# Weaving 18 of 32 gathers between the first six scatters on GpSimd

## The chip, the cores and the metric

One core of a Trainium2 chip runs the kernel. The metric is device time in microseconds (us), as the median of several executions. One more execution was taken with the hardware profiler; its trace is what all rows below come from.

## What is computed

The input `x` is 16 images of 128 channels and 16 x 16 pixels, so 4096 tokens of 128 numbers.

```python
x = x + einsum('oc,bchw->bohw', W, _ln_c(x))      # W from 32 Householder vectors
t = _to_tokens(x)                                  # 4096 tokens
xf = _ln_t(t)
Sm = softmax(xf @ W_router + b_router)             # 32 experts
G_ek, idx_ek = top_k(Sm.T, 128)                    # each expert takes its 128 best tokens
tokens = xf[idx_ek]
act = silu(einsum(tokens, W_up[group]) + b_up)     # 8 groups of 4 experts, width 341
Eout = einsum(act, W_down[expert]) + b_down
y = zeros.at[idx_ek].add(G_ek * Eout)              # tokens can be taken by several experts
out = _from_tokens(t + y)
```

## The kernel before

All arithmetic is in one program with five instruction streams (SyncE, GpSimd, ScalarE, VectorE, TensorE), ordered by semaphores alone; each stream is written out by hand and executes in its order.

The first part, up to about 67 us of the trace, makes the convolution, both normalisations, the softmax and the threshold of each expert. It leaves the normalised tokens with their 32 gate values in a DRAM table `token_rows` of 4096 rows of 160 floats, and two DRAM tables `acc0` (the residual) and `acc1` (zeros).

The second part goes over the 32 experts.

- TensorE finds the token numbers of an expert with a small matmul (`find`, L1152), VectorE turns its result into `idx[:, e]` (`token_number`, L944 and L946). The first 16 are made in a row; the other 16 are made four at a time between later units.
- GpSimd gathers the 128 rows of expert `e` from `token_rows` with an indirect DMA (`gather`, L523) into its own slot `xg[:, e, :]`; the slot of one expert is never used by another. It waits for `idx` of that expert alone.
- The experts are worked in nine units: experts 0-1, 2-3, and then 4-7, 8-11, 12-15, 16-19, 20-23, 24-27, 28-31. Of each unit TensorE transposes the gathered rows (`gathered_transpose`, L1164, after the wait for all gathers of the unit), multiplies with the up weights (`up`, L1178) and with the down weights (`down`, L1194). ScalarE copies the transposed rows (L650) and applies silu (L659). VectorE multiplies the down result with the gate and leaves `eo[:, e, :]`, which is the space of `X` (L991).
- The results of experts 0 to 25 (`SCATTERED` = 26) go back by an indirect DMA of GpSimd that adds to DRAM (`scatter`, L532), in turn into `acc1` and `acc0`. Scatter `e` waits for `eo` of its expert and for the landing of all earlier scatters to the same table, which is that of `e - 2`.
- The results of experts 26 to 31 go back through TensorE: VectorE makes a one-hot matrix of the token numbers for each (`token_onehot`, L956, four pieces each), and TensorE multiplies it with three bf16 parts of the result into all eight PSUM banks (L1216, 6 experts x 24 matmuls).

The end: when the scatters to `acc1` have landed, ScalarE's queue starts four loads of it (L663); when both tables are complete, SyncE's queue starts the other loads (L453, L454). VectorE adds the two tables chunk by chunk (L1001, eight chunks), TensorE transposes each sum onto the accumulated banks (L1221), ScalarE copies the banks out (L666), SyncE stores them (L457, L460).

On TensorE the order of a step `k` is `up(k + 1)`, `gathered_transpose(k + 2)`, `down(k)`; after the last `down` come L1216 and L1221. On VectorE the multiplications L991 of a unit come after the `token_number` calls of the next unit's finds, and pieces of L956 stand between them.

What sets the order on GpSimd in the second part is `AHEAD`: `AHEAD` gathers are issued before the first scatter. Before, `AHEAD` is 32, so all gathers come first and then the 26 scatters.

Of the kernel before, what the change touches and what calls it, by code (L numbers as in the profile page):

```python
# [10 lines left out]
E = 32  # L11
# [57 lines left out]
HOT_AFTER = (10, 17, 25)  # L69

INTO = tuple((SCATTERED - 1 - e) % 2 for e in range(SCATTERED))
AHEAD = E
EARLY = 4


# [50 lines left out]
def metaformer_block(nc, x, V, w_router, b_router, w_up, b_up, w_down, b_down, c32, c16, ch16, ccol, out):  # L126
# [7 lines left out]
    with ctx:  # L134
# [329 lines left out]
        def _(pool):  # L464
# [56 lines left out]
            def gather(e):  # L521
                pool.wait_ge(s_idx, e + 1)
                nc.gpsimd.indirect_dma_start(  # L523
                    out=xg[:, e, :], out_offset=None, in_=rows[:, :],
                    in_offset=bass.IndirectOffsetOnAxis(ap=idx[:, e:e + 1], axis=0)).then_inc(s_g[UNIT_OF[e]], 16)

            def scatter(e):
                pool.wait_ge(s_eo, e + 1)
                i = INTO[e]
                if e >= 2:  # L530
                    pool.wait_ge(s_sc[i], 16 * INTO[:e].count(i))
                nc.gpsimd.indirect_dma_start(  # L532
                    out=acc[i][:, :], out_offset=bass.IndirectOffsetOnAxis(ap=idx[:, e:e + 1], axis=0),
                    in_=eo[:, e, :], in_offset=None, compute_op=ALU.add).then_inc(s_sc[i], 16)
# [7 lines left out]
                in_offset=bass.IndirectOffsetOnAxis(ap=row_number[:, 0:1], axis=0)).then_inc(s_first, 16)  # L542
            for e in range(AHEAD):
                if e == E - 1:
                    pool.wait_ge(s_first, 16)
                gather(e)
            e = 0
            while e < SCATTERED:
                scatter(e)
                e += 1  # L550
# [691 lines left out]
```

## Time and profile before

| | us |
|---|---|
| median of 3 runs | 196.4 (196.19 to 196.7) |
| profiled execution, its own time | 196.68 |
| span of its trace | 194.9 |
| TensorE busy | 139.9 (72% of the span) |
| GpSimd busy | 107.1 (55%) |
| VectorE busy | 108.9 (56%) |

The span runs from the first to the last instruction, and 1.8 us of the profiled execution's own time lie around it. Times in rows count from the span's start. In rows PE is TensorE, PEld its weight loads, DVE VectorE, ACT ScalarE, POOL GpSimd, SP SyncE. The mean granted clock of TensorE is 0.828 of full speed. A busy GpSimd says that it makes DMA descriptors; the transfer itself runs on the DMA engines afterwards.

### The profile page before, as it was taken

The page shows a single profiled execution, that of the slowest core. Times are in us where ns is not written, and L with a number is a line of the kernel's source. Part 1 is how long each engine was busy: PE and PEld are TensorE (multiplying, and loading weights), DVE is VectorE, ACT ScalarE, POOL GpSimd, SP SyncE. Part 2 cuts the span into 40 slices and gives each one's busy share as a digit, 9 for nine tenths or more (in the row PEclk, how much of TensorE's full clock was granted, in tenths as well). Part 3 has the DMA queues.
Part 4 walks back from the last instruction along what each step waited for, and adds up shares of the span by engine and source line. Part 5 has one row for each costly group of instructions (what it writes and reads, how often), then busy time and mean ns, then how long its engine had stood idle before and what let it go on. Part 6 is the DMA issues. An engine that isn't in the chain of part 4 may idle for free.

```text
span 194.9 us, 2467 instructions
## 1 busy us (share of the span) xinstructions
PE 139.9 (72%) x694; PEld 87.6 (45%) x697; DVE 108.9 (56%) x433; ACT 76.1 (39%) x266; POOL 107.1 (55%) x120
## 2 busy tenths in 40 slices
PE   0999965413215347754299997999974999999990
PEld 0557954301104224334134763777652344444690
DVE  2454998984676692110435448458399069945500
ACT  3166899536895675100234252335400000000161
POOL 2028478997560277774356377878768878600000
PEclk9999999955555555557579999999997599999997
DMA  4999999999867062222112223334343333399666
GB/s 96 300 335 309 293 294 208 249 403 285 221 185 217 17 265 70 64 62 60 31 36 50 50 54 42 31 27 40 27 42 28 27 32 39 28 290 344 240 212 222
DMA packets 31982, 28.39 MB, mean 146 GB/s; under 512 B 6784, under 2 KB 25680, under 8 KB 31840
## 3 DMA queue, kind: packets, MB, share of 16 engines
q1 hardware_dynamic: 25777, 22.74, 39.8%
q0 software_dynamic: 5328, 4.41, 15.3%
q10 hardware_dynamic: 864, 1.08, 1.7%
q8 instruction: 6, 0.10, 0.2%
q14 instruction: 7, 0.06, 0.1%
HBM read 17.61 MB, written 10.62 MB: 145 GB/s over the span
## 4 chain that ended last, share of the span: by engine, by line
PE 53%; DVE 14%; POOL 12%; another core or an unknown queue 7%; issue 6%; ACT 3%; DMA 2%; SPq 0%; POOLq 0%; DVEq 0%
PE PZ L1216 9%; PE PT L1178 7%; PE PM L1178 6%; PE PZ L1194 5%; PE PT L1216 4%; PE PM L1216 4%; POOL rs L493 4%; PE PM L1194 3%; POOL rs L486 3%; PE PT L1017 3%; DVE wdn L956 2%; POOL act L499 2%; PE PZ L1221 2%; PE PT L1164 2%
## 5 line engine op out<-in xcount | busy, mean ns | idle before, releaser
L532 POOL DMA_INDIRECT acc<-X,idx x26 | 40.8, 1567 | 12.2 <-issue 8.2
L523 POOL DMA_INDIRECT xg<-token_rows,idx x32 | 30.4, 951 | 21.0 <-issue 9.6
L956 DVE TENSOR_SCALAR_CACHE_REDUCE wdn<-wide,slot_token 128x1024 bf16<-128x1024 f16 x24 | 29.9, 1273 | 7.0 <-PE PZ L1216 7.0
L944 DVE TENSOR_SCALAR_CACHE_REDUCE junk<-PZ,k 128x128 f16<-128x128 f32 x24 | 8.3, 348 | 25.1 <-remote 13.2
L666 ACT ACTIVATE X<-PZ 128x512 f32<-128x512 f32 x4 | 2.4, 598 | 45.1 <-PE PZ L1221 45.1
L1065 PE MATMUL PZ<-stage_w,X 128*128 128x192 f32 x64 | 14.7, 382 | 6.9 <-DVE act L788 6.5
L1194 PE MATMUL PZ<-wdn,act 128*128 128x128 f32 x132 | 18.7, 290 | 1.0 <-DVE X L991 1.0
L1194 PEld LDWEIGHTS PZ<-wdn,act 128*128 128x128 f32 x132 | 17.3, 204 | 2.1 <-DVE X L991 1.4
L1178 PE MATMUL PM<-xgT,wup 128*128 128x512 f32 (+3 forms) x26 | 15.0, 667 | 3.6 <-issue 2.5
L659 ACT ACTIVATE act<-PT,bup 128x512 f32<-128x512 f32 (+3 forms) x14 | 9.0, 641 | 21.4 <-PE PT L1178 14.5
L1178 PE MATMUL PT<-xgT,wup 128*128 128x512 f32 (+3 forms) x28 | 16.4, 672 | 0.9 <-ACT xgT L650 0.9
L659 ACT ACTIVATE act<-PM,bup 128x512 f32<-128x512 f32 (+3 forms) x13 | 8.3, 637 | 21.0 <-remote 8.1
L1065 PEld LDWEIGHTS PZ<-stage_w,X 128*128 128x128 f32 x64 | 12.4, 224 | 8.3 <-DVE act L788 7.5
L1216 PE MATMUL PZ<-wdn,S 128*128 128x512 bf16 x47 | 14.2, 406 | 2.5 <-DVE X L991 2.5
L1152 PE MATMUL PZ<-cum,onehot 32*128 32x129 f16 x32 | 6.9, 256 | 11.1 <-DVE idx L946 6.0
L991 DVE TENSOR_SCALAR X<-PZ,xg 128x128 f32<-128x128 f32 x22 | 7.4, 348 | 12.0 <-PE PZ L1194 10.1
L1152 PEld LDWEIGHTS PZ<-cum,onehot 32*128 32x128 f16 x32 | 2.9, 96 | 23.9 <-issue 20.5
L588 ACT ACTIVATE act<-act,mn 128x32 f32<-128x32 f32 x32 | 9.8, 310 | 6.0 <-DVE mn L792 6.0
L751 DVE SCALAR_TENSOR_TENSOR x<-PZ,rs,xg 128x128 f32<-128x128 f32 x32 | 9.1, 343 | 4.3 <-PE PZ L1065 2.7
L493 POOL TENSOR_TENSOR rs<-ve,mhalf 128x4 f32<-128x4 f32 x8 | 8.1, 1007 | 3.7 <-DVE ve L773 3.7
L620 ACT ACTIVATE xf<-x,shift,rs 128x128 f32<-128x128 f32 x24 | 9.4, 483 | 0.0
L1001 DVE TENSOR_TENSOR x<-x,xf 128x512 f32<-128x512 f32 x8 | 5.5, 693 | 6.9 <-DMA x<-acc 6.9
(180 smaller groups left out, 280.2 us busy)
## 6 DMA issues: line engine op xcount, KB each, us to landing
X<-in_x SPq DMA_DIRECT2D x8, 256.0 KB, 5.3
acc<-zero SPq DMA_DIRECT2D x4, 512.0 KB, 6.7
acc<-x SPq DMA_DIRECT2D x8, 256.0 KB, 5.9
token_rows<-xf SPq DMA_DIRECT2D x8, 256.0 KB, 2.3
x<-acc SPq DMA_DIRECT2D x8, 256.0 KB, 5.8
out<-X SPq DMA_DIRECT2D x3, 512.0 KB, 3.6
wup<-in_L_ffn_W_up SPq DMA_DIRECT2D x1, 1364.0 KB, 7.8
wdn<-in_L_ffn_W_down SPq DMA_DIRECT2D x1, 1280.0 KB
```

What stands on the lines that cost most here:

```text
L493: link(nc.gpsimd.tensor_tensor(rs2[:, g, :], ve2[:, g, :], mhalf[:, :], ALU.pow))
L523: nc.gpsimd.indirect_dma_start(out=xg[:, e, :], out_offset=None, in_=rows[:, :], in_offset=bass.IndirectOffsetOnAxis(ap=idx[:, e:e + 1], a ...
L532: nc.gpsimd.indirect_dma_start(out=acc[i][:, :], out_offset=bass.IndirectOffsetOnAxis(ap=idx[:, e:e + 1], axis=0), in_=eo[:, e, :], in_off ...
L588: ins = nc.scalar.activation(pr[:, g, u, :], lg[:, g, u, :], ACT.Exp, bias=mn[:, g, u:u + 1], scale=-1.0, accum_out=sm[:, g, u:u + 1])
L620: ins = nc.scalar.activation(xf[:, t, :], x1[:, t, :], ACT.Identity, bias=shift2[:, g, u:u + 1], scale=rs2[:, g, u:u + 1])
L659: nc.scalar.activation(act[0:fn, k % 2, j, 0:n * P], src, ACT.Silu, bias=bup[0:fn, j, e0 // PER:e0 // PER + 1]).then_inc(s_act, 1)
L956: nc.vector.tensor_scalar(hot(k)[:, r], columns[:, r], slot_token[:, k:k + 1], None, ALU.is_equal, ALU.add, accum_out=found_in[:, k * HOT_ ...
L1065: ins = mm(PZ[:, 2 * (g % 2) + u // 2, (u % 2) * W_:(u % 2 + 1) * W_], X[:, g, u * P:(u + 1) * P], stage_w[:, :], start=True, stop=True)
L1152: mm(find_bank(e), onehot[r, g, :], cum[r, g, 0:P + 1], start=True, stop=True).then_inc(s_find, 1)
L1178: mm(dst, wup[:, e0 // PER, f0:f0 + fn], xgT[:, k % 2, 0:n * P], start=True, stop=True).then_inc(s_up, 1)
L1194: ins = mm(down_bank(e), act[0:rows_, k % 2, j, q * P:(q + 1) * P], w, start=(j == 0), stop=(j == 2))
L1216: ins = mm(out_bank(g), parts[j][:, k, :], hot(k)[:, g * 512:(g + 1) * 512], start=(k == 0 and j == 0), stop=False)
```

## The change

The gathers are no longer all issued first. GpSimd issues gathers 0 to 13, then scatter 0 and gathers 14, 15, 16, then scatter 1 and gathers 17, 18, 19, and so on up to scatter 5 and gathers 29, 30, 31; the 20 scatters 6 to 25 follow in a row. The gathers, the scatters and their own semaphore waits are the same instructions in another order. One wait is no longer issued: that of gather 31 for an earlier gather into the same slot (`s_first`), which stands in the first loop alone.

```diff
-AHEAD = E
+AHEAD = 14
+PER_SCATTER = 3
@@
             for e in range(AHEAD):
                 if e == E - 1:
                     pool.wait_ge(s_first, 16)
                 gather(e)
-            e = 0
+            e, ahead = 0, AHEAD
+            while ahead < E:
+                scatter(e)
+                for _ in range(PER_SCATTER):
+                    gather(ahead)
+                    ahead += 1
+                e += 1
             while e < SCATTERED:
                 scatter(e)
                 e += 1
```

## Rows read from the trace of the kernel before

**Rows 1.** The page, chain that ended last, share of the span by engine.
```profile
PE 53%; DVE 14%; POOL 12%; another core or an unknown queue 7%; issue 6%; ACT 3%; DMA 2%; SPq 0%; POOLq 0%; DVEq 0%
```

**Rows 2.** The chain in order of time: start us, us, what.
```profile
80.41 5.09 another core or an unknown queue
...
86.07 6.47 another core or an unknown queue
...
93.12 1.57 another core or an unknown queue
...
182.87 0.43 PE PZ L1216 x2
183.30 1.78 PE PZ L1221 x16
```

**Rows 3.** Timeline of POOL: start us, us, instruction, count, [idle before <-what ended it].
```profile
84.68 0.95 POOL L523 DMA_INDIRECT xg<-token_rows,idx  x1 [0.30 <-issue]
...
89.69 0.95 POOL L523 DMA_INDIRECT xg<-token_rows,idx  x1 [0.30 <-issue]
...
115.94 0.95 POOL L523 DMA_INDIRECT xg<-token_rows,idx  x1 [0.49 <-issue]
117.19 1.62 POOL L532 DMA_INDIRECT acc<-X,idx  x1 [0.31 <-DVE X L991]
...
168.28 1.55 POOL L532 DMA_INDIRECT acc<-X,idx  x1 [0.45 <-issue]
```

**Rows 4.** Lines L523 and L532: duration in ns (least/median/most), first and last start.
```profile
L523 POOL DMA_INDIRECT xg<-token_rows,idx x32: 943/948/1027, 68.4 to 115.9; - x32
...
L532 POOL DMA_INDIRECT acc<-X,idx x26: 1552/1552/1681, 117.2 to 168.3; - x26
```

**Rows 5.** Timeline of DVE, first gated results of the experts.
```profile
96.92 0.61 DVE L991 TENSOR_SCALAR X<-PZ,xg 128x128 f32<-128x128 f32 x2 [1.07 <-remote]
...
103.17 0.35 DVE L991 TENSOR_SCALAR X<-PM,xg 128x128 f32<-128x128 f32 x1 [0.16 <-PE PM L1194]
```

**Rows 6.** Timeline of PE from the first to the last transpose of gathered rows.
```profile
73.59 0.66 PE L1164 MATMUL PT<-k,xg 128*128 128x128 f32 x2 [1.06 <-DMA xg<-token_rows,idx]
...
87.32 2.77 PE L1194 MATMUL PZ<-wdn,act 128*128 128x128 f32 x12
...
96.31 2.08 PE L1178 MATMUL PT<-xgT,wup 128*128 128x512 f32 x2
...
105.11 1.12 PE L1178 MATMUL PT<-xgT,wup 128*128 128x512 f32 x2
...
107.50 0.66 PE L1164 MATMUL PT<-k,xg 128*128 128x128 f32 x4
...
121.62 0.60 PE L1164 MATMUL PT<-k,xg 128*128 128x128 f32 x4
...
127.46 0.60 PE L1164 MATMUL PT<-k,xg 128*128 128x128 f32 x4
...
133.31 0.60 PE L1164 MATMUL PT<-k,xg 128*128 128x128 f32 x4
```

**Rows 7.** DMA issues of 60 to 80 us: last number is median us from issue to landing.
```profile
xg<-token_rows,row_number POOLq DMA_INDIRECT x1, 2.8
```

**Rows 8.** Timelines of the queues of ACT and SP, then of DVE, at the end.
```profile
169.68 1.79 ACTq L663 DMA_DIRECT2D xf<-acc  x4
...
172.20 1.76 SPq L454 DMA_DIRECT2D x<-acc  x4
...
176.21 1.42 DVE L1001 TENSOR_TENSOR x<-x,xf 128x512 f32<-128x512 f32 x2 [3.52 <-DMA x<-acc]
...
184.45 0.69 DVE L1001 TENSOR_TENSOR x<-x,xf 128x512 f32<-128x512 f32 x1 [0.58 <-DMA x<-acc]
```

**Rows 9.** Stage 92 to 96: busy us and count of PE, PEld, DVE, ACT, POOL; clock; DMA share, GB/s.
```profile
92.00:96.00 4.00, 0.00 (x0) 0.00 (x0) 1.59 (x8) 1.02 (x2) 1.42 (x2) 0.69 0.08 20
```

## The prediction

> **What bounds the kernel now.** I read the chain that ended last first, then the timelines of GpSimd, TensorE and VectorE from 68 us on, then the queues at the end. TensorE has over half of the chain and GpSimd 12% [rows 1]; from 96 us on the chain is TensorE's, with short VectorE pieces, and it passes from the last one-hot matmul at 182.87 straight into the transposes of the sums at 183.30 [rows 2]. The reader is to see there that no scatter and no gather stands on that path.
>
> GpSimd is a second chain beside it. Its last scatter starts at 168.28 [rows 3], the loads start at 169.68 and 172.20, and the sums run from 176.21 to 184.45 + 0.69 = 185.14 [rows 8]. TensorE takes the first sum at 183.30; 16 transposes, two chunks, take 1.78 [rows 2], so it takes the eighth at 183.30 + 7 x 0.89 = 189.5. The first sum is there at about 176.9: 6.4 us of slack at the first chunk, 189.5 - 185.1 = 4.4 at the last. I call 4.4 the slack of the scatters.
>
> Ahead of 96 us stands something else: 5.09 + 6.47 + 1.57 = 13.1 us of the chain wait for a releaser that the profile can't name [rows 2]. TensorE's records say that the down matmuls of experts 0 and 1 ran at 87.32 to 90.09, but VectorE could use them only at 96.92 [rows 5, 6]. TensorE's completions reach the others up to 7 us after their modelled ends. In the first two thirds of this stretch GpSimd issues one gather every 1.25 us, without a gap, until 90.64 [rows 3].
>
> **The change, part by part.** No instruction is added. Moved are 18 gathers (14 to 31) and six scatters (0 to 5).
>
> 1. *Gathers 0 to 13.* Unchanged; the last starts at 84.68 [rows 3] and ends at 85.63.
>
> 2. *The new wait.* Scatter 0 needs the result of expert 0, ready at 96.92 + 0.35, about 97.3 [rows 5]. With some 0.3 for the wake (the gap that most instructions of GpSimd show [rows 3]) it starts at 97.55. Behind it on GpSimd stand gathers 14 to 31. Before, gathers 14 to 17 were out by 90.64, and the rest went as their numbers came, until 116.89. The pause of 11.9 us costs nothing by itself: the first waiter for gathers 14 and 15 is the transpose at 107.50 [rows 6].
>
> 3. *Gathers against the transposes that wait for them.* A gather takes 0.95 and a scatter 1.55 [rows 4], each with a gap of 0.30 [rows 3]; one group of a scatter and three gathers is 1.85 + 3 x 1.25 = 5.60. No scatter waits for a landing, since scatter e - 2 is two groups back, and the next results are there at 103.52 and later [rows 5]. So group j starts at 97.55 + 5.60 j, and its gathers 1.85, 3.10 and 4.35 later. Landing comes 2.8 after the start, the one gather whose landing the profile gives [rows 7].
>    - Gather 15: start 100.65, landed 103.45; used at 107.50 [rows 6]. Margin 4.0.
>    - Gather 19: 107.50, 110.3; before, its transpose was between those at 107.50 and 121.62, seven us from each: 114.5. Margin 4.2.
>    - Gather 23: start 97.55 + 16.8 + 1.85 = 116.20, landed 119.0; used at 121.62. Margin 2.6.
>    - Gather 27: 97.55 + 22.4 + 3.10 = 123.05, 125.85; 127.46. Margin 1.6.
>    - Gather 31: 97.55 + 28.0 + 4.35 = 129.90, 132.7; 133.31. Margin 0.6.
>
>    Each transpose still finds its rows: 0 on TensorE's path. Both ends: from below 0, as no transpose of these units waits for a gather before. From above, a landing of 3.9 (gather 1 started 1.25 after the first at 68.4 [rows 4], and TensorE was released at 73.59 [rows 6], beside a heavy load of the DMA engines) and 0.2 more per scatter (its steady period, next step, in place of 1.85): gather 31 lands at 129.90 + 1.2 + 3.9 = 135.0, 1.7 late. I take 0: the rows nearest to it, gap and landing, are those of undisturbed gathers, and the DMA engines are lightly loaded there.
>
> 4. *The other 20 scatters.* Before, 26 scatters started from 117.19 to 168.28 [rows 3]: 51.09 / 25 = 2.04 each, more than the 1.85 of the instruction, because each waits for the landing of the one two before. After, gather 31 ends at 130.85, scatter 6 starts at 131.15 and the 25th at 131.15 + 19 x 2.04 = 169.9. That is 1.6 later than 168.28: the six scatters that went forward saved less than the pause lost. The loads, and the last sum, move to 185.1 + 1.6 = 186.7, and TensorE needs it at 189.5. 2.8 of the slack stays: 0 on the path. If that cover were gone, each us of GpSimd would cost one.
>
> 5. *The dropped wait of gather 31* was met long before (its gather is the first of all): 0.
>
> 6. *Traffic.* Gathers and scatters now share 97 to 131 us; TensorE, VectorE and ScalarE move nothing through DMA there: 0, from below and above no more than step 3 has.
>
> Sum: 0 + 0 + 0. On the profiled execution that is 196.68, which stands 0.3 above the median of the runs shown; my forecast is between them, 196.5, with a range of its own of 195.9 to 197.2.
>
> The Trainium skill (page "DMA: Bandwidth & Descriptors", section "Anatomy of one DMA") gives a DMA of GpSimd a fixed 2.0 us plus its bytes over 436 GB/s, most of it the receipt behind the last byte. For the 80 KB of a gather that is an estimate of 2.2 us; counted from the end of the instruction it would land gather 31 at 133.05, 0.3 ahead of its use, where the row gives 0.6. It thins the margin and leaves the sum at 0.
>
> **Rivals.**
>
> *R1, the late completions go away (faster).* If the stretch of rows 2 hangs on the unbroken stream of gathers, the change cuts it: GpSimd falls silent at 85.63 instead of 90.64. For it: the waits end within 2 to 4 us of GpSimd's first rest, and the completions came some 5 us apart while it issued. Against: the same stream ran from 68.4 on [rows 4], and the first unnamed wait begins at 80.41, 12 us into it; and GpSimd's scatters, as dense, delay nothing later. Price: at least a part of the 5.0 us by which the rest comes earlier, 3.5 say; at most, the next up matmuls start at 90.1, where TensorE's queue was through, not at 96.3: 6.2. The clock adds to it: TensorE had nothing from 92 to 96, the clock fell (0.69 in that stage [rows 9]), and a pair of up matmuls took 2.08 at 96.31 against 1.12 at 105.11 [rows 6]; two pairs at that rate are 1.9. So 3.5 to 8.1 us less: 188.5 to 193, 191 as its middle. Gathers and scatters start as much earlier, so the margins of step 3 stay.
>
> *R2, the gathers come too late (slower).* Place: the transposes of experts 24-27 and 28-31. It decides when gather 31 lands more than 0.6 later than in step 3, which 0.03 us more on each of the 24 instructions does. Price: 0.5 to 1.7, so 197 to 198.2, and 197.9 as the time that I give it. For it: the margin shrinks from group to group, since a group of GpSimd (5.60) is slower per gather than TensorE's use. Against: durations of both instructions vary little [rows 4]. [...]
>
> *R3, the late completions last longer or come again (slower).* Now GpSimd is busy without a gap from 97.55 to 170, with three gathers of four instructions up to 131. If R1's cause is real but needs a long stream, a second stretch appears after 107 us: 3 to 8 us, 199.5 to 204.5. Against: it is one event in the trace.
>
> *R4, the tail decides (slower).* It does if the last scatter is over 4.4 us late; step 4 gives 1.6. Only scatters at over 2.18 us each would do it.
>
> **How the numbers follow.** Forecast 0.47, R1 0.24, R2 0.14, R3 0.06, R4 0.04; 0.05 for a small gain or loss from the phase of the clock, split evenly. No change is what lies within 0.3%, 0.6 us, about what runs of this kernel can tell apart. Faster: R1 with half of the rest and some edge of the forecast, 0.28. Slower: R2, R3, R4 and a half, less the part of R2 under 0.6 us: 0.25. Same: 0.47. The range leaves out the deepest fifth of R1 and what lies above R2: 190 to 199.
>
> **What would show it.** GpSimd starts scatter 0 at 97.5 behind a gap of 12 us, gather 31 near 129.9, the last scatter near 170; no transpose L1164 after 97 us waits for a DMA; the last sum ends near 186.7 and TensorE passes from L1216 to L1221 without a wait; the three unnamed waits stay near 13 us. Wrong would be: unnamed waits of another length (R1, R3), L1164 waiting for gathers (R2), or L1221 waiting for sums (R4).

## The result, and the profile after

The changed kernel takes 198.63 us (median of 5, 198.19 to 200.15) against 196.4 for the kernel before beside it (median of 5, 195.6 to 197.72): a ratio of 1.0115, 95% interval 1.007 to 1.016. It is slower by 2.2 us, and all of the interval lies beyond the 0.3% that I counted as no change: the forecast of no change was wrong, though the time is in its range. The profiled execution took 198.63, its span is 196.7, so 1.9 lie around it.

In the rows of after, lines of GpSimd stand one later than before (L524, L533) and all behind them seven later (L666 for L659, L951 for L944, L998 for L991, L1008 for L1001, L1171 for L1164, L1185 for L1178, L1228 for L1221).

The page of after: its first line, the granted clock in 40 slices of 4.9 us, and the chain by engine, which answers to [rows 1].
```profile
span 196.7 us, 2466 instructions
...
PEclk9999999985555555557999995899999699999999
...
PE 53%; DVE 13%; POOL 12%; issue 7%; another core or an unknown queue 6%; ACT 4%; DMA 2%; SPq 0%; POOLq 0%; DVEq 0%; ACTq 0%
```
The share of the unnamed releaser is hardly another (6% for 7%). The difference is where it stands, and the reader sees that only in the chain in time.

The chain of after from 100 to 125 us: start us, us, what.
```profile
107.91 1.44 another core or an unknown queue
109.40 1.42 another core or an unknown queue
...
111.43 7.35 another core or an unknown queue
118.87 0.70 ACT act L666
```
Before, the chain had nothing of this kind after 95 us [rows 2]. Now it waits there for 1.44 + 1.42 + 7.35 and a smaller piece of 0.73, 10.9 us.

GpSimd in after, timeline, columns as in [rows 3].
```profile
85.02 0.95 POOL L524 DMA_INDIRECT xg<-token_rows,idx  x1 [0.30 <-issue]
90.75 1.62 POOL L533 DMA_INDIRECT acc<-X,idx  x1 [4.79 <-DVE X L998]
...
123.87 0.95 POOL L524 DMA_INDIRECT xg<-token_rows,idx  x1 [0.30 <-issue]
...
164.51 1.55 POOL L533 DMA_INDIRECT acc<-X,idx  x1 [0.39 <-issue]
```
The pause behind gather 13 is 4.79 and not 11.9: scatter 0 starts at 90.75. From there to 128.6 us there is no gap but the 0.3 of every instruction, and everything stands 5 to 7 us earlier than I had it (90.75 for 97.55, 123.87 for 129.90, 164.51 for 169.9).

TensorE in after, timeline; it answers to [rows 6], and its last row to the last of [rows 2].
```profile
97.45 1.12 PE L1185 MATMUL PT<-xgT,wup 128*128 128x512 f32 x2
99.84 0.66 PE L1171 MATMUL PT<-k,xg 128*128 128x128 f32 x4
...
119.61 2.00 PE L1185 MATMUL PM<-xgT,wup 128*85 128x512 f32 x2 [4.94 <-ACT act L666]
121.41 1.06 PE L1171 MATMUL PT<-k,xg 128*128 128x128 f32 x4
...
136.52 0.60 PE L1171 MATMUL PT<-k,xg 128*128 128x128 f32 x4
...
185.02 1.95 PE L1228 MATMUL PZ<-k,x 128*128 128x128 f32 x16
```
Read these against [rows 6]: the up matmuls of experts 8 to 11 that stood at 105.11 stand at 97.45, 7.66 earlier; the transposes of 107.50 at 99.84, 7.66 earlier; those of 121.62 at 121.41, 0.2 earlier; those of 133.31 at 136.52, 3.2 later. So TensorE won 7.7 us by 100 us and lost 10.9 from there to 137.

The other side of it: ScalarE's silu and VectorE's first result in after, timelines.
```profile
88.61 0.47 ACT L666 ACTIVATE act<-PT,bup 128x256 f32<-128x256 f32 x1 [3.77 <-remote]
...
118.87 0.69 ACT L666 ACTIVATE act<-PM,bup 128x512 f32<-128x512 f32 x1 [7.44 <-remote]
```
```profile
90.13 0.64 DVE L998 TENSOR_SCALAR X<-PZ,xg 128x128 f32<-128x128 f32 x2
...
181.58 0.69 DVE L1008 TENSOR_TENSOR x<-x,xf 128x512 f32<-128x512 f32 x1 [0.59 <-DMA x<-acc]
```
Expert 0 is multiplied at 90.13, where it was 96.92 [rows 5]: the first late stretch ends 6.8 us sooner. At 118.87 ScalarE has waited 7.44 for something that the profile can't name, and TensorE waits 4.94 for ScalarE: a second late stretch.

Windows of after around it, columns as in [rows 9].
```profile
116.00:120.00 4.00, 0.39 (x1) 0.36 (x2) 2.88 (x7) 0.69 (x1) 3.08 (x4) 0.74 0.37 71
120.00:124.00 4.00, 4.00 (x15) 2.82 (x14) 0.35 (x2) 1.97 (x3) 3.09 (x4) 0.50 0.29 42
```
TensorE is empty from 116 to 120, and from 120 to 124 it is full at a granted clock of 0.50, the lower of its two levels (1.2 of 2.4 GHz), so the up pair took 2.00 us for the 1.12 of [rows 6]. The Trainium skill has this in the page "TensorE: Matmul & The Clock Gate", section "HAM oscillation": there the waits are for a DMA, and an engine kept waiting between stages gets its clock halved and begins the next one cold. The two rows agree, though the wait here is for ScalarE.

Less than 3.2 is left at the end. In the chain TensorE comes to the sums at 185.18 for 183.30 [rows 2]; in the timelines, which reckon a row's start a little earlier, it is 185.02 for 183.14. Either way it is 1.9 later, and the profiled executions differ by 1.95. The one-hot matmuls between took 33.48 us before (149.66 to 183.14) and 32.15 now (152.87 to 185.02). The windows of 4 us go with it: before, the clock was 0.52 from 148 to 152 and 0.63 from 152 to 156; now it is 1.00 and 0.57, so one of two slow windows is gone.

### The profile page after: what moved, and what is told of

Read it like the earlier page. It is cut to its first block, busy times and chain, and to the rows that moved or that the text cites. A ratio compares the mean times of both kernels' runs of the same rounds, so it can differ in the third digit from the quotient of the medians.

```text
span 196.7 us, 2466 instructions
## 1 busy us (share of the span) xinstructions
PE 139.6 (71%) x694; PEld 89.0 (45%) x697; DVE 108.9 (55%) x433; ACT 75.9 (39%) x266; POOL 107.8 (55%) x120
## 4 chain that ended last, share of the span: by engine, by line
PE 53%; DVE 13%; POOL 12%; issue 7%; another core or an unknown queue 6%; ACT 4%; DMA 2%; SPq 0%; POOLq 0%; DVEq 0%; ACTq 0%
PE PZ L1223 8%; PE PM L1185 7%; PE PZ L1201 6%; PE PT L1185 6%; PE PM L1223 4%; PE PT L1223 4%; POOL rs L494 4%; POOL rs L487 3%; PE PT L1024 3%; DVE wdn L963 2%; PE PT L1171 2%; PE PM L1201 2%; POOL act L500 2%; PE PZ L1228 2%
## 5 line engine op out<-in xcount | busy, mean ns | idle before, releaser
L533 POOL DMA_INDIRECT acc<-X,idx x26 | 41.1, 1582 | 16.1 <-DVE X L998 7.2
L524 POOL DMA_INDIRECT xg<-token_rows,idx x32 | 30.7, 959 | 12.3 <-issue 8.2
L1201 PE MATMUL PZ<-wdn,act 128*128 128x128 f32 x132 | 19.9, 303 | 1.0 <-DVE X L998 1.0
L1185 PE MATMUL PM<-xgT,wup 128*128 128x512 f32 (+3 forms) x26 | 15.1, 668 | 7.5 <-ACT act L666 4.9
L1201 PEld LDWEIGHTS PZ<-wdn,act 128*128 128x128 f32 x132 | 18.5, 217 | 2.1 <-DVE X L998 1.4
L951 DVE TENSOR_SCALAR_CACHE_REDUCE junk<-PZ,k 128x128 f16<-128x128 f32 x24 | 8.3, 347 | 19.7 <-remote 8.3
L666 ACT ACTIVATE act<-PT,bup 128x512 f32<-128x512 f32 (+3 forms) x14 | 9.0, 641 | 24.5 <-PE PM L1185 9.9
L1185 PE MATMUL PT<-xgT,wup 128*128 128x512 f32 (+3 forms) x28 | 15.4, 638 | 2.7 <-ACT act L666 1.7
L998 DVE TENSOR_SCALAR X<-PZ,xg 128x128 f32<-128x128 f32 x22 | 7.5, 348 | 16.1 <-PE PZ L1201 12.1
L666 ACT ACTIVATE act<-PM,bup 128x512 f32<-128x512 f32 (+3 forms) x13 | 8.3, 636 | 20.5 <-remote 13.2
L1223 PE MATMUL PZ<-wdn,S 128*128 128x512 bf16 x47 | 13.6, 390 | 2.5 <-DVE X L998 2.5
L1201 PE MATMUL PM<-wdn,act 128*128 128x128 f32 (+1 forms) x60 | 8.5, 278 | 2.1 <-DVE X L998 2.1
L1185 PEld LDWEIGHTS PM<-xgT,wup 128*128 128x128 f32 (+1 forms) x26 | 4.6, 212 | 10.7 <-ACT act L666 6.5
```

Of the source, the lines that this page charges most:

```text
L524: nc.gpsimd.indirect_dma_start(out=xg[:, e, :], out_offset=None, in_=rows[:, :], in_offset=bass.IndirectOffsetOnAxis(ap=idx[:, e:e + 1], a ...
L533: nc.gpsimd.indirect_dma_start(out=acc[i][:, :], out_offset=bass.IndirectOffsetOnAxis(ap=idx[:, e:e + 1], axis=0), in_=eo[:, e, :], in_off ...
L666: nc.scalar.activation(act[0:fn, k % 2, j, 0:n * P], src, ACT.Silu, bias=bup[0:fn, j, e0 // PER:e0 // PER + 1]).then_inc(s_act, 1)
L1185: mm(dst, wup[:, e0 // PER, f0:f0 + fn], xgT[:, k % 2, 0:n * P], start=True, stop=True).then_inc(s_up, 1)
L1201: ins = mm(down_bank(e), act[0:rows_, k % 2, j, q * P:(q + 1) * P], w, start=(j == 0), stop=(j == 2))
L1223: ins = mm(out_bank(g), parts[j][:, k, :], hot(k)[:, g * 512:(g + 1) * 512], start=(k == 0 and j == 0), stop=False)
```

## The experiments

Everything that I ran asks two questions: what makes the completions of TensorE late, and whether the order of gathers and scatters costs anything without that. Times are compared with runs of the kernel before on the same chip. The runs fall into five groups, each on one chip and at one time; I call such a group a session. A completion is late when ScalarE or VectorE gets on with the result of a matmul only microseconds after that matmul's recorded end, and the profile names no releaser; such waits in a row are a late stretch.

### The pause alone

```diff
             for e in range(AHEAD):
+                if e == 14:
+                    pool.wait_ge(s_eo, 1)
```


> Before's order with one wait added: gather 14 waits for the result of expert 0, then gathers 14 to 31, then the 26 scatters. It has the changed kernel's pause without its weaving. Theory S (stream): TensorE's completions come late once GpSimd has issued indirect DMAs with gaps of 0.30 us for some 11 us, and come right again within 3 us of a rest. Theory M (mix): the first late stretch is as in S, the second one of the changed kernel comes from scatters and gathers sharing the queue. Both expect the first late stretch to end near 88.6 us as in the changed kernel and scatter-free gathers from about 90.7. S expects a second late stretch that starts 10 to 12 us later, about 101, if gathers 14 to 27 run without gaps; M expects none, and then some 188 to 191 us. Theory P (place: what TensorE does there, whatever GpSimd does) has no reason for either.

Measured: 196.34 for 196.72 before, ratio 0.9941 (0.9888 to 0.9995). Chain of this kernel in time:
```profile
79.45 3.35 another core or an unknown queue
...
83.38 4.33 another core or an unknown queue
...
96.88 4.85 another core or an unknown queue
...
101.77 2.11 another core or an unknown queue
```
With the pause the first stretch ends early (expert 0 at 89.2), as in the changed kernel; so the pause alone brings the early end. GpSimd goes on at 89.82 with ten gathers without a gap, and a second stretch stands from 96.88 to 104.6, some 4 us sooner than S had it, though no scatter is in the stream. That a second stretch needs a mix of gathers and scatters is refuted. Behind it GpSimd has to wait for token numbers several times (0.8 to 3.5 us between 102 and 113) and no lateness comes again, which fits that this kernel's time is not above the one before.

### A rest earlier

```diff
+                if e == 8:
+                    pool.wait_ge(s_idx, 17)
```


> Before's order with one wait added: gather 8 waits for the index of expert 16, a rest of about 2 us for GpSimd near 78.5 to 80.7 us. S: the first late stretch no longer begins near 80; expert 0's result is there at about 87 (before 97), and a late stretch begins 10 to 12 us after the rest, near 91 to 92, if the stream is unbroken till then. P: the late stretch begins near 80 as before, and its end stays near 97. S gives 190 to 197 us in all, P 196 to 197.

Measured: 196.08, ratio 0.995 (0.9896 to 1.0005). Timelines of ScalarE and of GpSimd:
```profile
82.99 0.47 ACT L661 ACTIVATE act<-PM,bup 85x256 f32<-85x256 f32 x1 [0.82 <-PE PM L1180]
...
93.41 0.68 ACT L661 ACTIVATE act<-PT,bup 85x512 f32<-85x512 f32 x1 [2.11 <-remote]
```
```profile
80.00 0.94 POOL L523 DMA_INDIRECT xg<-token_rows,idx  x1 [2.10 <-DVE idx L948]
...
98.86 0.95 POOL L523 DMA_INDIRECT xg<-token_rows,idx  x1 [0.30 <-issue]
```
One rest of 2.1 us at 77.9 takes the stretch at 80 away: silus that were late before are released by name, within 1 us. A new stretch starts at about 87.5, 7.5 us after the stream went on (S had 10 to 12), and lasts to 103: the down matmuls of expert 2 end at 91.71, and VectorE is released by them at 102.57, 10.9 later. So the lateness isn't bound to a place in TensorE's work; it comes some time after the start of an unbroken stream of GpSimd's DMAs.

### A rest at every unit, in both orders

In the order before, and in the changed order, the first gather of each unit waits for the landing of the unit before (2.3 to 3.6 us of rest behind every four gathers, two in the first units; one of the changed order's boundaries has none, as a scatter stands there).

```diff
+                u = UNIT_OF[e]
+                if u >= 1 and e == UNITS[u][0]:
+                    pool.wait_ge(s_g[u - 1], 16 * UNITS[u - 1][1])
```


> Before's order, but the first gather of each unit waits until the gathers of the unit before have landed: a rest of 1.5 to 2 us after every four gathers (after every two in the first two units). S: no late stretch at all if such rests are enough; up matmuls of the third unit start near 87 instead of 96.3, the clock stays up, TensorE's chain is 9 to 11 us shorter. The gathers end near 117 as before or earlier, so the scatters end near 170 and the last sum near 185: the scatters then set the end, and the whole is 193 to 196 us. P: late stretch from 80 as before, 196 to 197.

> The changed kernel with the same rests: the first gather of each unit waits until the unit before has landed. Rests of 1.5 to 2 us stand after gathers 1, 3, 7, 11, 15, 23 and 27; before gather 20 stands a scatter. S: neither late stretch, or short ones; TensorE's chain 9 to 11 us shorter than in the kernel before; the scatters end near 162 to 166 and the whole is 187 to 192 us. M: the second late stretch (101 to 129) stays, since gathers and scatters still share the queue: 190 to 199.

Measured: 202.2, ratio 1.0307 (1.0241 to 1.0374), and 202.22, ratio 1.0263 (1.0182 to 1.0344). Both are longer than any time expected of them. From 78 us on, where the late stretches stood, neither trace has an unnamed wait of VectorE or ScalarE up to 140 us or in its chain. The first kernel is slower all the same, for another reason:
```profile
185.52 3.78 PE L1224 MATMUL PZ<-k,x 128*128 128x128 f32 x16 [9.49 <-DVE x L1004]
```
TensorE is through its one-hot matmuls at 176.0, 7.3 earlier than before, and then waits 9.49 for the sums, since the scatters ended at 178.3. The slack of the scatters (4.4 in the prediction) is what the rests use up. In the second the mix of gathers and scatters runs without lateness, but TensorE waits for gathers (3.14 at 101.08, 3.04 at 119.26, 2.95 at 137.34; its transposes stand 9 us apart, where the last ones before were 5.9 apart).

### Two gathers under way at most, and few rests, in a session without lateness

Each gather has its own semaphore. In two kernels (old order, changed order) every gather waits for the landing of the one two before:

```diff
+                if e >= 2:
+                    pool.wait_ge(s_g[e - 2], 16)
```


> Before's order; each gather counts on a semaphore of its own and waits for the landing of the gather two before it, so a gather starts every 1.45 to 1.6 us in place of 1.25, with a gap of 0.5 to 0.6 in place of 0.30 and no long rest. Theory R (rate): what delays TensorE's completions builds up while indirect DMAs start faster than something drains, so a slightly slower even rate is enough: no late stretch, third unit's up matmuls near 87 to 90, TensorE 8 to 10 us earlier through the middle, and then the scatters (issued until about 173) set the end: 194 to 198 us. Theory G (gap): only a rest of 1.5 us or more helps: late stretch from about 82 on, about as long as before, 196 to 201 us.

> The changed kernel's order with the same rule: a gather waits for the landing of the gather two before it. In a group the gap grows to 0.5 to 0.6 only at some gathers (the scatter between gives the landing its time), so the woven stream starts a DMA every 1.5 us on the mean against 1.43. R: the first late stretch goes, the second gets shorter or goes: 190 to 196. G: both stay: 198 to 202.

In a third, in the changed order, there are three rests:

```diff
# in gather(e)
+                if e in (8,):
+                    pool.wait_ge(s_g[e - 1], 16)
# in scatter(e)
+                if e in (2, 4):
+                    pool.wait_ge(s_g[AHEAD - 1 + PER_SCATTER * e], 16)
```


> The changed kernel's order with three rests for GpSimd (gather 8 waits for the landing of gather 7, scatter 2 for that of gather 19, scatter 4 for that of gather 25), so no unbroken run of indirect DMAs is over 11 us. Theory S (an unbroken run of 8 to 11 us makes TensorE's completions late, a rest of about 2 us ends that): no late stretch or only traces of one; TensorE's one-hot matmuls end near 172 to 178 instead of 185; the last scatter starts near 166 to 168 and the sums end near 183, so the scatters set the end: 189 to 193 us, faster than both kernels. If the mix of gathers and scatters is what hurts, the second late stretch stays: 196 or more.

In a fourth, `AHEAD` is 16, `PER_SCATTER` 4, and the rests are before gather 8 and scatters 0, 1 and 3.

> 16 gathers first, then one scatter and four gathers in turn four times, then the other 22 scatters, with rests before gather 8 and scatters 0, 1 and 3. Longest unbroken runs: 10, 10, 7, 14 and 7 us. S: at most a late stretch near 113 to 118, in the run of 14 us; gather 31 lands near 123, about when TensorE wants it; scatters end near 166: 189 to 195 us.

Measured: 201.3, 199.61, 191.12 and 192.29, with ratios of 1.0974 (1.091 to 1.1038), 1.0844 (1.0792 to 1.0896), 1.0382 (1.0336 to 1.0429) and 1.0474 (1.0423 to 1.0525). The ratios are large because the kernel before took 183.98 (7 runs, 183.38 to 184.55) here, where it had taken 196.72 in the first four comparisons. No expectation foresaw that. All four show no lateness, but by its time the kernel before had none here either; so they tell nothing of what prevents it, and the question whether a slower rate alone would do (two gathers under way) stays open. They do price the rests where they buy nothing: 7 us for three, 8 for four, 16 to 17 for a landing awaited at each gather. The price shows on TensorE: with three rests its transposes wait for gathers for 4.18 at 111.91 and 0.95 at 127.99, and with a landing awaited at each gather in the old order it waits 8.51 for the sums at the end.

### Both kernels again, unchanged

> The kernel before, unchanged, for its trace beside the times of its own group. In the group of the last four runs it took 184.0 us where it takes 196.4 to 196.7 in the others. If TensorE's late completions are what differs between groups, this trace shows them exactly where its time is near 196.5, and none (no wait of DVE or ACT over 1 us for an unnamed releaser between 79 and 97) where it is near 184; then a lack of late completions in a kernel of that group says nothing on its rests.

> The changed kernel, unchanged, in the same group. If the group has no late completions: scatter 0 near 87, gather 31 near 119.2, the last scatter starts near 159, TensorE's chain ends as the one of before, 184 us, the same as before within 0.5 us (my first forecast's sum of three zeros, free of the late stretches). If the group has them: 198 to 199, with late stretches from 80 to 88.6 and from 101 to 129 again.

Measured on one chip: the kernel before 184.96 (10 runs), and beside it 185.0 (19 runs), ratio 1.0009 (0.9956 to 1.0061); the changed kernel 184.68 (10 runs), ratio 0.9998 (0.9953 to 1.0044). The kernel before here, VectorE and GpSimd:
```profile
85.48 0.35 DVE L991 TENSOR_SCALAR X<-PZ,xg 128x128 f32<-128x128 f32 x1 [1.01 <-PE PZ L1194]
```
```profile
68.11 0.97 POOL L523 DMA_INDIRECT xg<-token_rows,idx  x1 [2.92 <-DVE idx L941]
...
106.84 0.95 POOL L523 DMA_INDIRECT xg<-token_rows,idx  x1 [0.30 <-issue]
```
All 32 gathers run from 68.11 to 107.79 without a gap, longer than any unbroken stream in the traces of the two kernels above (the changed kernel's, 90.75 to 128.6, is 38 us), and nothing is late: expert 0 is there at 85.48, not 96.92 [rows 5], released by a named matmul after 1.01. Not one unnamed wait stands in the chain from 64 to 125 us. With TensorE 12.9 us earlier (its first one-hot matmul starts at 136.72 for 149.66) the end is another one, though:
```profile
175.55 2.43 PE L1221 MATMUL PZ<-k,x 128*128 128x128 f32 x16 [0.16 <-DVE x L1001]
```
The last scatter starts at 159.72 and the last sum ends at 176.76, so TensorE's last transposes wait for the sums. From 124 us on the chain runs over scatters, loads and sums, and of the slack of 4.4 nothing is left. The changed kernel here: TensorE's transposes and its first transposes of sums, then the last piece of the chain on this stretch.
```profile
107.48 0.66 PE L1171 MATMUL PT<-k,xg 128*128 128x128 f32 x4 [1.76 <-DMA xg<-token_rows,idx]
...
114.40 0.66 PE L1171 MATMUL PT<-k,xg 128*128 128x128 f32 x4 [0.85 <-DMA xg<-token_rows,idx]
...
121.34 0.66 PE L1171 MATMUL PT<-k,xg 128*128 128x128 f32 x4 [0.87 <-DMA xg<-token_rows,idx]
...
171.37 1.95 PE L1228 MATMUL PZ<-k,x 128*128 128x128 f32 x16
```
```profile
118.73 2.56 DMA xg<-token_rows,idx
```
Scatter 0 starts at 85.63 and the mix of gathers and scatters runs without a gap to 123.5, with nothing late in it. But GpSimd is now the slower of the two, and R2 is there: the last three units (experts 20 to 31) wait 1.76 + 0.85 + 0.87 = 3.5 us for their gathers. Gather 31 starts at 118.73 and lands 2.56 later at 121.29, and the last transposes stand at 121.34, where the kernel before had them at 120.37. Its first one-hot matmul starts at 137.76 for 136.72, 1.0 later. TensorE had been 3.1 ahead at 92.63 (for 95.75), with a clock of 1.00 from 80 to 92 us for 0.76; the waits used that up. The lead is not the change's: TensorE has 3.1 already at 83.33 (for 86.45), before GpSimd issues its first moved instruction at 85.63, and its up matmuls near 79 take 0.70 a pair for 1.22 at the lower clock. The scatters end at 160.2 and the last sum at 175.48, 1.3 earlier than in the kernel before, and the end has no wait: TensorE starts on the sums at 171.37 for 169.45, 1.9 later, and is through at 178.67 for 177.98. So what the late gathers cost is in part hidden, since the kernel before has to wait for its sums. In the times the difference is -0.02%, to within 0.5%, so a loss of 0.7 us is hidden in it.

Two things follow: an unbroken stream is not enough to cause late completions, and without them the 1.15% of the result are not there. With them, the unchanged pair was timed in one session only, that of the result.

### The three rests where completions are late

The kernel with three rests again, and one with a single rest (scatter 2 waits for gather 19's landing).

> The same kernel as the one with three rests, in another group. If the group has late completions (before near 196.5): no unbroken run is over 11 us, so no or only short late stretches, 190 to 193 us, 2 to 3% faster than before. If it has none (before near 184.5): the rests only cost, 191 as in the earlier group, 3.8% slower than before.

> The changed kernel with one rest: scatter 2 waits for the landing of gather 19. In a group with late completions: the first late stretch to 88.6 as in the changed kernel, the second begins near 101 and is cut by the rest at about 102 to 105, a third may begin 8 to 10 us later: 191 to 197 us. In a group without: 185 to 187, the rest costs TensorE at most its 2 us.

Measured, beside 196.79 for the kernel before (8 runs, 196.34 to 197.39): three rests 191.49, ratio 0.9714 (0.9659 to 0.9769); one rest 195.53, ratio 0.9929 (0.9878 to 0.9981). Of the second only the time is read here. Chain of the first:
```profile
89.07 2.81 another core or an unknown queue
...
92.50 3.67 another core or an unknown queue
```
The rests do not take everything away: GpSimd ran from 80.41 to 99.05 without a gap, since scatters 0 and 1 were ready early, and a stretch stands from 87 to 99; its last late release, at 99.04, comes as GpSimd falls silent. From the rest at 99.05 to 101.43 on nothing is late. So the same kernel that loses 3.8% where nothing is late wins 2.9% where something is. No kernel that I tried is shown to beat the one before in both situations.

## Why the prediction was right in its range and wrong in its mechanism

The 198.63 us lie in the range of 190 to 199, 0.4 below its end, and outside the 195.9 to 197.2 that the forecast itself had. They lie so near to no change by luck: the forecast added up zeros, while a gain of 7.7 us and a loss of 10.9 nearly cancelled.

*Step 1* held: the last of the first 14 gathers starts at 85.02, for 84.68.

*Step 2* failed, and first of all. "The pause of 11.9 us costs nothing by itself" left out what a silent GpSimd does to the others. The pause was 4.79 long and it brought a gain: the kernel with the pause alone has the short first stretch too (expert 0 at 89.2). I had this as R1, with 0.24 and a price of 3.5 to 8.1 us; the up matmuls of experts 8 to 11 came 7.66 earlier, within it. The reason I had set against it, that the stream had run 12 us before the first wait, was in truth how this lateness behaves: it sets in some 7 to 12 us after GpSimd begins an unbroken run (12 after 68.4, 7.5 after 80.0, about 8 after 89.8, about 11 after 90.75).

*Step 3*, whether gathers come in time, gave the right sum for the profiled run of the changed kernel. What L1171 waited for there (us, times):
```profile
  DMA xg<-token_rows,idx: 1.0, 1
```
The one time is the first unit's. But this was no proof of the margins, as TensorE was late itself at 113 to 119. The raster is slower than in the sum: gather 31 starts 33.12 after scatter 0, for 5 x 5.60 + 4.35 = 32.35, so a group takes 5.73 and not 5.60 (the scatter 1.62, the first gather behind it 0.99). That alone is 0.77, more than the margin of 0.6 that I gave gather 31. Where nothing is late, the three waits above are the outcome: R2 at its place and one unit sooner, with the last transposes 1.0 us later, of its 0.5 to 1.7. The landing was taken well: 2.56 after the start, for 2.8. That is 1.6 after the end of the instruction, where the other estimate of the prediction had 2.2 from there. I had written that 0.03 us on each of 24 instructions decides it and still gave it 0.14; it deserved the even chance that a margin of the size of its own error has.

*Step 4* held. The last scatter started at 164.51, 40.64 after gather 31, for 169.9 - 129.9 = 40.0. Here the last sum ends at 181.58 + 0.69 = 182.27, 2.75 before TensorE starts on the first; R4 did not occur. But the slack of 4.4 was that of a TensorE held up by late completions; where it isn't, the kernel before has none left.

*Steps 5 and 6*: no row contradicts them. Without lateness the two kernels' times differ by 0.0% within 0.5%, but by two effects and not by zeros: gathers later, and scatters that were on the path earlier.

*The rivals* are the second failure. R1 and R3 were given as alternatives, 0.24 and 0.06, and both came true in one run: the pause ended the first stretch, and by that GpSimd stood at 90.75 with 18 gathers and six scatters in hand whose token numbers and results were all ready. Before, gathers from 18 on had waited for numbers that were themselves late; those waits were rests. Timeline of GpSimd before:
```profile
93.39 0.95 POOL L523 DMA_INDIRECT xg<-token_rows,idx  x1 [2.75 <-issue]
```
Others of 1.09 to 2.38 us follow up to 112.0. The changed kernel has no gap above 0.31 until 128.6, and the second stretch came. I had written "it is one event in the trace" against R3, and had not asked what the gain of R1 would do to GpSimd's own gaps. A row on GpSimd's gaps between 93 and 112 was what the argument lacked. -7.7, +10.9, and -1.3 at the later fall of the clock are the +1.9 at L1228.

What is shown: the pause brings the gain (alone, it does too); a second stretch needs no scatter; in the sessions with lateness it appears with unbroken streams and not in the kernels with a rest at each unit; in runs without lateness the change makes no difference that can be measured, with late gathers in the trace. What is not shown: what in the chip delays the completions, why they are late in one session and not in the next, and what ends a stretch: in the changed kernel the second one lets up near 121 (a silu at 121.65 follows its matmuls at once) and ends near 129, with no gap of GpSimd above 0.55 by then. Each of these readings rests on one trace of its kernel. The same chip had both (196.72 and 183.98 for the same kernel, at two times).

## What to carry to other kernels

A wait named by no releaser, on a single core, is worth asking after before any change is priced: a stream beside it may cause it, and then a pause is a gain and a faster stream is a loss. When a rival removes a stall, work out what the engines do with the time, for the condition of the stall may come back later. And a kernel whose time hangs on such an effect should be timed in more than one session: an edit that won 2.9% in one lost 3.8% in another.

## What the runs showed of the hardware

The unchanged kernel took 196.4, 196.72 and 196.79 us in three sessions and 183.98 and 185.0 in two others, with single runs within some 2 us of these. In the two traces of it the difference is late completions of TensorE and what follows them: 9.9 of the 12.9 us by which the first one-hot matmul moves are there when the stretch ends (up matmuls at 96.31 and 86.45), and 1.9 go with the lower clock behind it. By TensorE's rows the down matmuls of expert 0 were through at about 90, VectorE was released at 96.92 [rows 5, 6]; without lateness VectorE follows within about a microsecond. The window rows fit that the matmuls were done: TensorE had 0.00 us of work from 92 to 96, at a clock of 0.69 [rows 9].

In the sessions with lateness the last late release came at 96.92 with GpSimd's first gap at 90.64 (before), at 88.65 with 85.97 (changed), at 87.73 with 85.15 (pause alone), at 102.57 with 99.81 (a rest earlier), and at 99.04 with 99.05 (three rests). The changed kernel's second stretch ended without such a gap. Eight rests of 2.3 to 3.4 us, one ahead of each unit's gathers, left no stretch.

An indirect DMA costs GpSimd the same wherever it stands: 0.95 for a gather (0.99 to 1.00 behind a scatter) and 1.55 to 1.62 for nearly every adding scatter, with 0.30 between two when nothing has to be waited for; mixed in groups of one and three, 5.73 us.
